# First attention of a decoder layer: queries projected two heads at a time, rotated ahead of the scores, and scores that contract over 64 rows in two row halves of the array

## The reference, cut to what matters

```python
q = _apply_rope(q, cos, sin)          # t * cos + rotate_half(t) * sin
k = _apply_rope(k, cos, sin)
q1, q2 = (q[..., :SUB], q[..., SUB:]) # SUB = 64
k1, k2 = (k[..., :SUB], k[..., SUB:])
s1 = einsum('bhqd,bhkd->bhqk', q1, k1) * scale
s2 = einsum('bhqd,bhkd->bhqk', q2, k2) * scale
a1, a2 = softmax(masked s1), softmax(masked s2)
diff = relu(a1 - lam * a2)
diff = diff / (sum(diff) + 1e-06)
out = einsum('bhqk,bhkd->bhqd', diff, v)
```

## Time and profile before

| | |
|---|---|
| median of 3 runs | 1567.81 us (1566.16 to 1569.45) |
| profiled execution: span | 1567.8 us, nothing around it |
| TensorE busy | 1482.3 us, 95% of the span |
| VectorE, ScalarE, GpSimd busy | 936.7, 724.9, 274.6 us |
| first attention | from the start to about 560 us |
| chain that ended last | PE 75%, issue 10%, DVE 7%, ACT 4%, POOL 3% |

### The profile page before, as it was taken

How to read it: one execution, slowest core, us unless ns; L and a number is a source line. 1 busy time by engine, 2 the same in 40 slices (tenths; PEclk the granted TensorE clock), 3 DMA queues, 4 the chain that set the end, 5 groups by cost and what they waited for, 6 DMA issues and landing times.

```text
span 1567.8 us, 24333 instructions
## 1 busy us (share of the span) xinstructions
PE 1482.3 (95%) x8196; PEld 1131.9 (72%) x8196; DVE 936.7 (60%) x2020; ACT 724.9 (46%) x2760; POOL 274.6 (18%) x243
## 2 busy tenths in 40 slices
PE   5899999999998789999999999978999999999998
PEld 4788888788887655666666666656777777777776
DVE  7888888788778655445445445544555455445454
ACT  2677667666776544344343443443233232322323
POOL 3232132113112211111111111231001020100201
PEclk9999999999999899999999999967999999999999
DMA  4000000000010001001001001001001010010100
GB/s 175 1 1 22 1 1 22 3 1 1 1 65 20 7 1 64 1 1 64 1 1 64 0 0 59 1 1 59 1 1 60 1 59 0 0 59 0 59 27 27
DMA packets 9696, 36.44 MB, mean 23 GB/s; under 512 B 2816, under 2 KB 7296, under 8 KB 8192
## 3 DMA queue, kind: packets, MB, share of 16 engines
q1 hardware_dynamic: 9600, 35.22, 6.2%
HBM read 33.12 MB, written 2.10 MB: 22 GB/s over the span
## 4 chain that ended last, share of the span: by engine, by line
PE 75%; issue 10%; DVE 7%; ACT 4%; POOL 3%; DMA 0%; DVEq 0%; POOLq 0%; SPq 0%; ACTq 0%
PE ps L381 31%; PE ps L746 10%; PE ps L666 4%; PE ps L561 4%; PE ps L564 4%; PE ps L495 3%; PE ps L640 3%; PE ps L521 3%; PE ps L656 2%; PE ps L773 2%; ACT ea L1276 2%; POOL ea L1512 2%; PE ps L648 1%; PE ps L512 1%; PE ps L436 1%
## 5 line engine op out<-in xcount | busy, mean ns | idle before, releaser
L1242 ACT ACTIVATE pt<-ps 128x512 f32<-128x512 f32 x128 | 76.7, 599 | 272.2 <-PE ps L505 139.8
L1276 ACT ACTIVATE ea<-ps,negmax 128x128 f32<-128x128 f32 x512 | 179.4, 376 | 19.5 <-DVE negmax L955 19.5
L1004 DVE TENSOR_TENSOR qcs<-ps,tabb 128x512 f32<-128x512 f32 x192 | 123.7, 686 | 81.0 <-PE ps L381 80.5
L1205 DVE TENSOR_TENSOR hu<-ps,sg 128x512 f32<-128x512 f32 x100 | 69.2, 692 | 168.9 <-PE ps L381 166.6
L1242 ACT ACTIVATE hhh<-hh 128x512 fp32r<-128x512 f32 x100 | 63.2, 632 | 227.4 <-DVE hh L1210 227.4
L381 PE MATMUL ps<-xnh,wch 128*128 128x512 f32 x400 | 160.3, 401 | 0.5 <-DVE x_sb L917 0.5
L381 PE MATMUL ps<-xnh,wcl 128*128 128x512 f32 x400 | 160.3, 401 | 0.0
L381 PE MATMUL ps<-xnl,wch 128*128 128x512 f32 x400 | 159.3, 398 | 0.0
L495 PEld LDWEIGHTS ps<-kva,qab 128*128 128x128 f32 x1024 | 139.7, 198 | 6.5 <-issue 1.5
L495 PE MATMUL ps<-kva,qab 128*128 128x128 f32 x1024 | 139.4, 280 | 1.2 <-issue 1.2
L1512 POOL TENSOR_TENSOR eb<-eb,rsum 128x512 f32<-128x512 f32 x64 | 66.6, 1041 | 389.4 <-DVE rsum L1042 389.4
(11 more groups left out here) (153 smaller groups left out, 3725.4 us busy)
## 6 DMA issues: line engine op xcount, KB each, us to landing
raw_w<-in_rawc_dram SPq DMA_DIRECT2D x6, 2240.0 KB, 8.4
raw_w<-in_rawb_dram SPq DMA_DIRECT2D x4, 2432.0 KB, 9.0
raw_a<-in_wqk_dram SPq DMA_DIRECT2D x4, 768.0 KB, 4.6
x_sb<-x_dram SPq DMA_DIRECT2D x4, 512.0 KB, 7.5
raw_w<-in_wo_dram SPq DMA_DIRECT2D x1, 2048.0 KB, 11.1
out<-x_sb SPq DMA_DIRECT2D x4, 512.0 KB, 2.9
wv<-in_wv_dram SPq DMA_DIRECT2D x1, 512.0 KB, 7.4
kvin<-ctx_in_dram SPq DMA_DIRECT2D x1, 512.0 KB, 4.5
```

The source lines that it names most:

```text
L1004: last = dve.tensor_tensor(quads(qcs[:, t, m, :]), quads(bk), bcast(tabb[:, t % 3, m, :]), ALU.mult)
L1205: dve.tensor_tensor(hu[:, par, :], bank(C_U[par]), sg[:, par, :], ALU.mult).then_inc(c_hu, 1)
L1242: return act.activation(dst, src, ACT.Copy)
L1276: last = act.activation(dst(m, h), quads(src)[:, h, :], ACT.Exp, bias=negmax[:, par, i:i + 1], accum_out=sums[:, par, i:i + 1])
```

## The change

A query item now holds the same half (rows 0 to 63 or 64 to 127 of the head) of two heads, one in rows 0 to 63 of the array and one in rows 64 to 127: tile (p, m) is half m of heads 2p and 2p+1. VectorE multiplies each item by cos/8 and by sin/8 (tables that it scales once at the start), and GpSimd finishes the rotation with two 128x512 instructions a pair (`a_queries`: `qrot` minus or plus `qcross`), four more instructions a chunk. The keys are the same in both row halves. A score matmul contracts over 64 rows: head 2p in rows 0 to 63 into one bank, head 2p+1 in rows 64 to 127 into the other, in turn. TensorE waits for the rotated queries (a_q) once a chunk, ahead of the scores at j = 0. The number of matmuls and of their columns, and of VectorE's and ScalarE's instructions, stays as it was. `a_keys` moves from j = 0 to j = 1, `a_queries` stands at j = 2 and j = 3 (`a_rotate`). The values' item moves from place 4 to the last, so from slot 0 of j = 2 to slot 1 of j = 3; q2 and q3 move up to slots 0 and 1 of j = 2. Since the values are the last item, the keys' item of the next chunk waits for a_vf.

```diff
 
-        qab = sb(am, "qab", [128, 2, 2, HG, CW])
+        qab = sb(am, "qab", [128, 2, 2, HG // 2, 2, CW])
+        qrot, qcross = qab[:, :, 0, :, :, :], qab[:, :, 1, :, :, :]
         ea = sb(am, "ea", [128, 2, 2, HG, S])
...
 
-        A_ITEMS = ["k", "k'", "q0", "q1", "v", "q2", "q3"]
+        A_ITEMS = ["k", "k'", "q0", "q1", "q2", "q3", "v"]
         AN, AV = len(A_ITEMS), A_ITEMS.index("v")
...
             return item - (item > AV)
+
+        def a_columns(ap, tile):
+
+            if tile < 2:
+                return ap[:, :, 128 * tile:128 * (tile + 1)].rearrange("p k (i d) -> p k i d", i=2)
+            p, m = (tile - 2) // 2, (tile - 2) % 2
+            return ap[:, :, 256 + 256 * p:512 + 256 * p].rearrange("p k (i m d) -> p k i m d", i=2, m=2)[:, :, :, m, :]
+
+        def a_block(ap, tile):
+
+            return ap[:, :, 128 * tile:128 * (tile + 1)].rearrange("p k (i d) -> p k i d", i=2)
 
...
                         pe.wait_ge(a_k, g * NC + (c + 1))
+                        pe.wait_ge(a_q, HG // 2 * (g * NC + (c + 1)))
                     wait(pe, a_ex, n - 1)
                     tok = slice(S * j, S * (j + 1))
-                    for m in range(2):
-                        sc = quads(A_S[u % 2][:, m, :])
-                        pe.matmul(sc, idb[:, :], maskb[:, :].unsqueeze(1).broadcast_to([128, HG, S]),
+                    for i in range(2):
+                        pe.matmul(quads(A_S[u % 2][:, i, :]), idb[:, :],
+                                  maskb[:, :].unsqueeze(1).broadcast_to([128, HG, S]),
                                   start=True, stop=False, skip_group_check=True)
-                        for h in range(HG):
-                            last = pe.matmul(sc[:, h, :], qab[:, c % 2, m, h, tok], kva[:, c % 2, m, tok],
-                                             start=False, stop=h == HG - 1, skip_group_check=True)
+                    for k in range(HG):
+                        p, m = k // 2, k % 2
+                        for i in range(2):
+                            half = slice(64 * i, 64 * i + 64)
+                            last = pe.matmul(A_S[u % 2][:, i, S * k:S * (k + 1)], qrot[half, c % 2, p, m, tok],
+                                             kva[half, c % 2, m, tok], start=False, stop=k == HG - 1,
+                                             skip_group_check=True)
                     last.then_inc(a_sc, 1)
...
             pe.wait_ge(a_vf, 1)
+            pe.wait_ge(a_pf, 5)
             pe.wait_ge(s_cst, 2)
...
                 if item == 0:
-                    to = ((kva[:, par, 0, :], 2), (kva[:, par, 1, :], 5))
+                    to = ((kva[:, par, 0, :], 4), (kva[:, par, 1, :], 5))
                 elif item == 1:
                     wait(dve, a_k, chunk)
-                    to = ((ktmp[:, 0, :], 3), (ktmp[:, 1, :], 4))
+                    to = ((ktmp[:, 0, :], 5), (ktmp[:, 1, :], 4))
                 else:
-                    h = a_tile(item) - 2
-                    to = ((qab[:, par, 0, h, :], 0), (qab[:, par, 1, h, :], 1))
+                    p, m = (a_tile(item) - 2) // 2, (a_tile(item) - 2) % 2
+                    to = ((qrot[:, par, p, m, :], 0), (qcross[:, par, p, m, :], 1))
                 for i, (dst, tab) in enumerate(to):
...
             dve.wait_ge(a_tab, 16)
+            dve.tensor_scalar(taba[:, 0:2, :], taba[:, 4:6, :], 0.125, None, ALU.mult).then_inc(a_t8, 1)
             ln_norm(1)
             dve.wait_ge(s_const, 16)
             dve.wait_ge(s_mask, 16)
             dve.tensor_copy(idb[:, :], idf[:, :]).then_inc(s_cst, 1)
             dve.tensor_copy(maskb[:, :], maskf[:, :]).then_inc(s_cst, 1)
+            dve.wait_ge(a_t8, 1)
             for item in A_START[0]:
...
                         i = m * HG + h
-                        src = (A_S[par][:, m, :] if maps == 2 else B_S[par])
-                        last = act.activation(dst(m, h), quads(src)[:, h, :], ACT.Exp, bias=negmax[:, par, i:i + 1],
+                        k, at = (h % 2, 2 * (h // 2) + m) if maps == 2 else (0, h)
+                        src = (A_S[par][:, k, :] if maps == 2 else B_S[par])
+                        last = act.activation(dst(m, h), quads(src)[:, at, :], ACT.Exp,
+                                              bias=negmax[:, par, HG * k + at:HG * k + at + 1],
                                               accum_out=sums[:, par, i:i + 1])
...
                 def slot(s):
+                    item = A_SLOT.get((j, s))
+                    ahead = not drain and item is not None and not (final and c == NC - 1)
+                    if ahead and item == AV:
+                        a_take_v(g + 1 if c == NC - 1 else g, (c + 1) % NC)
+                    elif ahead and c == NC - 2 and not final:
+                        act.wait_ge(a_pj, (g * NC + (NC - 1)) * AN + (item + 1))
+                        a_high(g + 1, a_tile(item))
                     for what in A_EXTRA.get((a_part(first, final, drain), u, s), []):
...
                             last.then_inc(b_kvc, 1)
-                    if drain or (j, s) not in A_SLOT or (final and c >= NC - 2 and not (c == NC - 2 and A_SLOT[j, s] == AV)):
-                        return
-                    item = A_SLOT[j, s]
-                    if item == AV:
-                        a_take_v(g + 1 if c == NC - 1 else g, (c + 1) % NC)
-                    elif c == NC - 2:
-                        act.wait_ge(a_pj, (g * NC + (NC - 1)) * AN + (item + 1))
-                        a_high(g + 1, a_tile(item))
                 slot(0)
...
                 pool.wait_ge(a_hi, g_to * AW + (tile + 1))
-                t = slice(128 * tile, 128 * (tile + 1))
-                pool.tensor_tensor(wal[:, :, t], raw_a[:, :, t], wah[:, :, t].bitcast(f32), ALU.subtract)\
-                    .then_inc(a_lo, 1)
+                pool.tensor_tensor(a_block(wal, tile), a_columns(raw_a, tile), a_block(wah, tile).bitcast(f32),
+                                   ALU.subtract).then_inc(a_lo, 1)
 
             def a_keys(g_to, c):
 
                 pool.wait_ge(a_pf, (g_to * NC + c) * AW + 2)
                 for m in range(2):
-                    last = pool.tensor_tensor(kva[:, c % 2, m, :], kva[:, c % 2, m, :], ktmp[:, m, :], ALU.add)
+                    last = pool.tensor_tensor(kva[:, c % 2, m, :], kva[:, c % 2, m, :], ktmp[:, m, :],
+                                              (ALU.subtract, ALU.add)[m])
                 last.then_inc(a_k, 1)
+
+            def a_queries(g_to, c, p):
+
+                pool.wait_ge(a_pf, (g_to * NC + c) * AW + (4 + 2 * p))
+                for m in range(2):
+                    last = pool.tensor_tensor(qrot[:, c % 2, p, m, :], qrot[:, c % 2, p, m, :],
+                                              qcross[:, c % 2, p, 1 - m, :], (ALU.subtract, ALU.add)[m])
+                last.then_inc(a_q, 1)
+
+            def a_rotate(g_to, c, j):
+
+                if j == 1:
+                    a_keys(g_to, c)
+                elif j:
+                    a_queries(g_to, c, j - 2)
 
...
                 if final and c >= NC - 2:
-                    if u == UN - 2 * CB:
-                        a_keys(g, NC - 1)
+                    if c == NC - 2:
+                        a_rotate(g, NC - 1, j)
                     return
-                if j == 0:
-                    a_keys(g + 1 if c == NC - 1 else g, (c + 1) % NC)
+                a_rotate(g + 1 if c == NC - 1 else g, (c + 1) % NC, j)
                 if c == NC - 2:
...
             a_keys(0, 0)
+            a_queries(0, 0, 0)
             ln_low(1)
+            a_queries(0, 0, 1)
             ln_rstd(2)
```

5 lines of the change are left out of this document (2 added, 3 removed).

## The result

The changed kernel takes 1651.02 us (median, 1649.05 to 1652.33) against 1568.05 for the kernel before, a ratio of 1.0532 (95% interval 1.0517 to 1.0547): 83 us slower. The forecast was 1636 us, range 1592 to 1676. The profiled execution spans 1648.1 us.

What follows compares the result with a forecast made beforehand. TensorE was taken to set the pace, the VectorE-ScalarE ring a tenth behind. Changed: 35.2 us a chunk, 145.8 a group against 124.2; 65 for groups 0 to 2, plus 8, minus 5, is 68: 1636 us, range 1592 to 1676.

Steps and rivals of the forecast that it cites:

- the ring: VectorE and ScalarE, negmax to negmax: 7.48 us a turn with an item in slot 0, 6.45 without; 28.9 a chunk after.
- rival "faster": New work meets nothing, rotations and values' copy cost no time: 28.9 us a chunk, about 1544 us; chance 0.11.
- The hold-up of VectorE: GpSimd's rotations delay ratio, rho and difference: 1.15 us each in j = 1 and 2, 2.1 in j = 3.
- the values' stall alone: Rival: VectorE's hold-up is small, the late values' copy real: 30.8 us a chunk, about 1572 us; chance 0.05.
- The values' stall: At j = 0 the next chunk's k item waits for ScalarE's copy behind eight exps: turn 1.95 us longer, once a chunk.
- the loop's jump: The jump now hides in the stall of the values; 5 us taken off for it and the first units together.
- hold-up alone: Rival: ScalarE copies the values in time, but GpSimd still holds up VectorE: 33.3 us a chunk, about 1610; chance 0.09.
- The row halves: Score matmuls in two row halves run side by side: 0.89 us a unit saved, TensorE needs 26.7 us a chunk.
- That the pairing brings nothing: Rival: row halves save nothing, TensorE stays at 30.3 us a chunk, sum moves 8 us or less; with clock 0.17.
- The third chunk: Splitting the next group's weights among rotations holds up more difference instructions: 5 us more a group, range 2.4 to 8.
- the last group: Three chunks with items, no weights to split, next stage's layer norm: about 3 us each, 8 in all, an estimate.
- the low clock: Rival: k item behind the stall at 1.2 GHz, 18 us more, 1654; with row halves, on top of stalls, 0.17.

Runs made afterwards that it cites:

- e2: Changed kernel with GpSimd's rotations of a unit started only after VectorE's four difference instructions of that unit: 1576.20 us, ratio 1.0050 to the kernel before.
- e3: Also e3_both: changed kernel with both repairs, rotations behind the difference and values copied ahead of the exps: 1550.14 us, ratio 0.9886 to the kernel before.
- e1: Changed kernel with ScalarE copying the values ahead of the unit's eight exps at j = 3: 1630.68 us, ratio 1.0407 to the kernel before.
- e4: Kernel before with only the item order changed, values last and copied behind the exps of j = 3: 1591.67 us, ratio 1.0145.
- e8: Changed kernel with both repairs, plus eight spare mask matmuls before TensorE's wait for the output weights' low halves: 1546.83 us, ratio 0.9870 to the kernel before.

## Why the prediction was right

The forecast was 1636 us and 1651.0 were measured, inside the range. The forecast's increase was 68 us and the measured one 83.

**The bound before, and the ring.** Right. Without hold-ups the turns of e2 and e3 are 7.37 to 7.41 us with an item and 6.45 without, where the prediction had 7.48 and 6.45. The two repairs end near its rival "faster" (1544, measured 1550), which supposed just that.

**The hold-up of VectorE.** Right in mechanism, place and size: 1.17 us measured for 1.15 in j = 1 and 2, 2.15 for 2.1 in j = 3. Taking it away gives 75 us, where the sum had 66; the prediction's rival with the values' stall alone, at 1572, was measured as e2, 1576. The Trainium skill, page SBUF — State Buffer, section Who interferes with whom, says that an instruction of VectorE with two inputs in SBUF contends with one of GpSimd that reads SBUF. The rows here agree: `ratio` takes 1.26 us instead of 0.15, while an item (one input in PSUM) takes 0.69 us beside a rotation, and `negmax` takes 1.22 beside one in e2, both as without it. The prediction took that `ratio` might slip through in j = 3; it did not.

**The values' stall.** Right in mechanism: the turn of j = 0 is 9.52 us where nothing else disturbs it (predicted 9.43), TensorE's wait 1.94. In the total it was too high: 15 times 1.95 us are 29, the removal gave 20 from the changed kernel and 26 from e2 (1576.2 to 1550.1), and its addition to the kernel before cost 24. In two chunks of four it lies on top of another wait. The prediction had guessed this for the loop's jump alone and took off 5 us for it and the start together. For the semaphore it took 0.1 us; from the copy's end at 326.72 to the k item at 326.76 are 0.04. The rival "hold-up alone" at 1610 was measured as e1, 1631.

**The row halves.** They pair, as the prediction took it, but give less. From the first score matmul of a unit to the transposes behind them are 1.09 us (330.04 to 331.13), where sixteen full ones took 1.78: 0.69 us a unit are saved and not 0.89, and TensorE needs 27.5 us a chunk by the prediction's own sum and not 26.7. That the pairing brings nothing is refuted by 1.16 us against 1.71. That TensorE would not be the limit in the changed kernel, so that the sum moves by 8 us or less, was measured as about 9.

**The third chunk.** The term was a little small: its four turns take 10.64, 10.46, 10.89 and 9.74 us, 41.7 together against 35.3 for the plain ones, 6.4 more where 5 were taken. 1.1 of it is the low clock behind the values' stall, shown above. The low parts of the weights stand in front of `norm` and the rotations there, and `norm` starts 1.0 us behind `rec` instead of 0.8 ahead of it, so that the difference instructions get caught:

```profile
281.49 0.72 POOL L1518 TENSOR_TENSOR wal<-raw_a,wah 128x256 fp32r<-128x256 f32 x1 [6.00 <-ACT wah L1262]
282.17 1.04 POOL L1547 TENSOR_TENSOR ea<-ea,rden 128x512 f32<-128x512 f32 x1
283.17 2.60 POOL L1533 TENSOR_TENSOR qab<-qab 128x512 f32<-128x512 f32 x2
```

```profile
282.26 3.91 DVE L918 SCALAR_TENSOR_TENSOR ea<-ea,rho 128x128 f32<-128x128 f32 x4
```

Four instructions, 1.14 us when undisturbed, take 3.91. By their own times three of them are caught, one by `norm` (1.09 us) and one by each rotation (1.36 and 1.35), and the fourth takes its 0.34 us when GpSimd is done (these two fences are timelines of the changed kernel, GpSimd and VectorE).

**The remaining 15 us** between forecast and result. From the first `rec` of a group to that of the next, in the two profiled executions:

| group | before | changed | more | forecast |
|---|---|---|---|---|
| 0 | 127.2 | 147.5 | 20.2 | 21.6 |
| 1 | 127.6 | 150.2 | 22.6 | 21.6 |
| 2 | 124.0 | 150.0 | 26.0 | 21.6 |
| 3 (to its last `rec`) | 135.7 | 151.8 | 16.0 | 8 |
| all else | | | -4.5 | -5 |
| together | | | 80.4 | 68 |

The largest error is the last group, for which the prediction had only an estimate: 16 us more and not 8. 6.3 of them are one turn, 15.33 us where it was 9.01 before. The projection bank explains it. The next stage's layer norm uses it right behind the values, so that its transposes (L400) also wait until ScalarE, behind its eight exps, has copied the values:

```profile
586.49 0.64 ACT L1262 ACTIVATE kva<-ps 128x512 f32<-128x512 f32 x1
587.23 1.09 PE L400 MATMUL ps<-idf,xnt 128*128 128x128 f32 x4 [5.60 <-issue]
```

The profile names no releaser, but the transposes start about 0.1 us behind the copy in this kernel, in e4 (after 3.39 us of idle time) and in e3_both (after 0.73), where the copy stands ahead of the exps. The turn is 11.42 us with the values taken early (e1), 12.76 with the rotations moved (e2) and 8.29 with both. So it is the values' stall once more, drawn out by the hold-up of VectorE ahead of the exps, in a place where the prediction did not look for it.

Groups 0 to 2 gave 69 us where 65 were forecast. The group around the jump took 150.7 us and not 145.8. Of these 4.9 us the wait for the output weights with the low clock behind it is 1.5 (10.20 and 9.45 against 8.58 and 9.52), the third chunk 1.7 (its turns are 10.87, 10.77, 10.57 and 9.75 us here, the first with the low clock), and the loop's jump 1.1 (10.24 and 9.02 against 9.52 and 8.60); the rest is small surpluses. In the first two of these a part is the low clock, a rival of the prediction, which put it at every k item; behind the values' stall it comes in the third chunk alone. The jump did hide, in part: the kernel before pays some 3 us for it, which is why group 1 gained less than group 2. The last 3 us of the 15 are the difference between the profiled executions and the medians. All this is addition from rows and no experiment of its own.

## What to carry to other kernels

Before an idle GpSimd is given work, look at which VectorE instructions with two SBUF inputs run at that moment: here each waited for the end of the GpSimd instruction under way, and small ones lost the most (0.15 us became 1.26). Here a semaphore that puts the same work 1.7 to 2.7 us later turned 1651 us into 1576. When the sequence on one engine is changed, look at each consumer's place in its own queue too (a copy behind eight exps), and at everything else that uses the same bank (the next stage's transposes), and count a stall once where it lies on top of others. And a saving on the engine that was the limit is worth only the distance to the next ring: here that was a tenth by the prediction's sum.

## What was not expected of the hardware

- A waiting instruction of VectorE gets in between two back-to-back instructions of GpSimd. Each small one thus pays for the rest of one GpSimd instruction, a whole one where they follow each other: 0.15 us became 1.26 and 1.19 in a row, and four difference instructions, three of them caught, went from 1.14 to 3.91 us together.
- GpSimd hardly pays in turn: its pair takes 2.49 to 2.51 us with `ratio` and `rho` waiting, 2.60 with the difference instructions waiting, and 2.53 alone.
- Matmuls over 64 rows in alternating row halves start in pairs: sixteen in 1.16 us; with one half ahead of the other, 1.71.
- Two waits of TensorE, 1.90 and 1.07 us with two matmuls of 512 columns between, and the granted clock stands at 0.50 in the 5 us around and behind the second. Behind a single wait of 1.9 to 2.0 us, for the values' copy or (with both repairs) for the output weights, it fell in some places of a run and not in others; with the wait filled it stayed at 1.00 in three of three places of e8.
